# A batched lambda layer on Trainium2: the query matmul in quarters of the array, and one sum for all of them

## What is computed

```python
keys = xf @ Wk.T
softmax_keys = jax.nn.softmax(keys, axis=1)
values = _bn(xf @ Wv.T, gamma_v, beta_v, axes=(0, 2), ch_shape=(1, -1, 1))
queries = (xf @ Wq.T).reshape(b, n, k_dim, h).transpose(0, 2, 1, 3)
queries = _bn(queries, gamma_q, beta_q, axes=(0, 2, 3), ch_shape=(1, -1, 1, 1))
content_lambda = jnp.einsum('bmk,bmv->bkv', softmax_keys, values)
position_lambdas = jnp.einsum('nmk,bmv->bnkv', E, values)
content_output = jnp.einsum('bknh,bkv->bhvn', queries, content_lambda)
position_output = jnp.einsum('bknh,bnkv->bhvn', queries, position_lambdas)
return (content_output + position_output).reshape(b, d, n1, n2)
```

## Time and profile before

| | |
|---|---|
| median of 3 runs | 1535.9 us (1535.89 to 1537.47) |
| profiled execution | 1534.77 us, its span 1533.0 us |
| mean granted TensorE clock | 0.992 |
| PE / DVE / POOL / ACT busy | 1478.9 / 1004.7 / 681.2 / 420.0 us |

### The profile page before, as it was taken

The page is one execution under the profiler, slowest core; times in us unless marked ns, Lnnn a source line. Parts: engine busy times, 40 slices in busy tenths (PEclk is TensorE's granted clock), DMA queues, the critical chain, the costliest instruction groups (busy, mean ns, idle before and its releaser), DMA issues.

```text
span 1533.0 us, 28096 instructions
## 1 busy us (share of the span) xinstructions
PE 1478.9 (96%) x10443; PEld 1237.9 (81%) x10443; DVE 1004.7 (66%) x1416; ACT 420.0 (27%) x721; POOL 681.2 (44%) x524
## 2 busy tenths in 40 slices
PE   6886989999999999999999999999999999999997
PEld 6885768888888888888888888888888888888886
DVE  5769876666666666666666666666666666666663
ACT  4664322222222222222222222222222222222220
POOL 6663264444444444444444444444444444444441
PEclk9998999999999999999999999999999999999999
DMA  8744411625324341526233343416253243424221
GB/s 276 251 134 100 86 56 35 118 62 107 69 62 89 89 89 54 90 62 116 62 89 62 89 89 79 92 34 116 62 109 69 62 89 89 89 57 86 62 55 27
DMA packets 338460, 134.68 MB, mean 88 GB/s; under 512 B 202640, under 2 KB 333824, under 8 KB 337920
## 3 DMA queue, kind: packets, MB, share of 16 engines
q1 hardware_dynamic: 338432, 134.31, 39.4%
HBM read 109.12 MB, written 25.17 MB: 88 GB/s over the span
## 4 chain that ended last, share of the span: by engine, by line
PE 92%; DVE 5%; POOL 2%; issue 1%; ACT 0%; DMA 0%; DVEq 0%; SPq 0%; POOLq 0%; ACTq 0%
PE ps_a L1096 78%; PE ps_b L1113 8%; PE ps_b L989 3%; PE ps_a L979 1%; PE ps_a L1080 1%; DVE bn L676 1%; DVE q_stats L697 1%; POOL q_diag L475 0%; DVE e_lo L710 0%; DMA x_main<-in_x 0%; DVE v_nat L882 0%; DVE bn L679 0%; POOL s_buf L460 0%; DVE v_stats L691 0%; DVE pos L805 0%
## 5 line engine op out<-in xcount | busy, mean ns | idle before, releaser
L1096 PE MATMUL ps_a<-v_hi,e_hi 128*128 128x512 f32 x1736 | 683.1, 393 | 6.1 <-DVE pos L805 5.9
L1096 PE MATMUL ps_a<-v_hi,e_lo 128*128 128x512 f32 x1736 | 676.7, 390 | 0.0
L1096 PEld LDWEIGHTS ps_a<-v_hi,e_hi 128*128 128x128 f32 x1736 | 326.4, 188 | 76.5 <-issue 6.6
L1096 PE MATMUL ps_a<-b_lo,e_hi 128*128 128x512 f32 x992 | 386.5, 390 | 0.0
L1096 PEld LDWEIGHTS ps_a<-v_hi,e_lo 128*128 128x128 f32 x1736 | 326.6, 188 | 66.1
L569 ACT ACTIVATE e_hi<-e_nat 128x512 fp32r<-128x512 f32 x310 | 196.2, 633 | 595.2 <-PE ps_a L1096 588.5
L475 POOL TENSOR_TENSOR q_diag<-qn,row_mask 128x1024 f32<-128x1024 f32 x128 | 254.4, 2009 | 206.2 <-PE ps_b L1113 205.0
L471 POOL TENSOR_TENSOR e_nat<-e_nat,s_buf 128x512 f32<-128x512 f32 x62 | 81.0, 1306 | 523.5 <-DVE e_lo L705 523.5
L705 DVE TENSOR_TENSOR e_lo<-e_nat,e_hi 128x512 fp32r<-128x512 f32 x310 | 295.1, 952 | 0.3
L1096 PE MATMUL ps_a<-t_lo,e_hi 128*128 128x512 f32 x744 | 290.2, 390 | 0.0
L772 DVE TENSOR_TENSOR pos<-ps_a,content 128x512 f32<-128x512 f32 x186 | 128.7, 692 | 175.0 <-PE ps_a L1096 172.7
(11 more groups left out here) (126 smaller groups left out, 862.9 us busy)
## 6 DMA issues: line engine op xcount, KB each, us to landing
e_nat<-in_L_conv_E SPq DMA_DIRECT2D x128, 512.0 KB, 4.9
res<-in_x SPq DMA_DIRECT2D x64, 256.0 KB, 6.7
out_dram<-res SPq DMA_DIRECT2D x64, 256.0 KB, 4.8
x_main<-in_x SPq DMA_DIRECT2D x24, 512.0 KB, 4.6
q_dram<-q_nat SPq DMA_DIRECT2D x4, 2048.0 KB, 7.8
q_blk<-q_dram SPq DMA_DIRECT2D x32, 256.0 KB, 5.3
x_more<-in_x SPq DMA_DIRECT2D x8, 512.0 KB, 9.0
gam_q<-in_L_conv_gamma_q SPq DMA_DIRECT2D x8, 0.1 KB, 8.0
```

The lines of the kernel that those rows point to most:

```text
L1096: ins = nc.tensor.matmul(BANK_OF[i], e[:, i, j].rearrange("p n k -> p (n k)"), v[:, j], start=(STARTS[i] and j == 0 and n == 0), stop=(STO ...
```

## The change

The query takes one image in a matmul: 32 weight columns of `pos`, 32 columns of `q_diag`, in the quarter a of the array. There are 64 matmuls a pair instead of 32. Each result is wanted whole, and is written to columns (t, g) of its quarter of partitions, so that all results of a pair fill 512 columns of one PSUM bank, in the same order in all four quarters. `add_out` then makes one sum over 128 partitions instead of four over 32, except for the last pair, where four sums stay.

```diff
--- before.py
+++ after.py
@@ -810,15 +810,11 @@
                 if new_block:
                     dve.wait_ge(res_loaded, (p // PPB) * (16 * A) + 16 * A)
                 dve.wait_ge(queried, p + 1)
-                for a in range(A):
-                    rows = slice(a * V, (a + 1) * V)
-                    r = res[rows, :, bass.ds((p % (2 * PPB)) * (2 * TN), 2 * TN)].rearrange("v f (t n) -> v f t n", t=2)
-                    s = ps_b[rows, 0].rearrange("v (t a f n) -> v a f t n", t=2, a=2, n=TN)[:, a % 2]
-                    ins = nc.vector.tensor_tensor(r, s, r, ALU.add)
-                    if each:
-                        ins.then_inc(res_added, 1)
-                if not each:
-                    ins.then_inc(res_added, 1)
+                r = res[:, :, bass.ds((p % (2 * PPB)) * (2 * TN), 2 * TN)].rearrange("v f (t n) -> v f t n", t=2)
+                s = ps_b[:, 0, 0:BANK].rearrange("v (t f n) -> v f t n", t=2, n=TN)
+                for a in range(A if each else 1):
+                    rows = slice(a * V, (a + 1) * V) if each else slice(0, P)
+                    nc.vector.tensor_tensor(r[rows], s[rows], r[rows], ALU.add).then_inc(res_added, 1)
 
             def lam_scale():
                 dve.wait_ge(lam_summed, 1)
@@ -1106,10 +1102,9 @@
                     pe.wait_ge(res_added, p)
                 for t in range(2):
                     for g in range(G):
-                        for half in range(2):
-                            cols = slice(g * P + half * HALF, g * P + (half + 1) * HALF)
-                            to = ps_b[half * HALF:(half + 1) * HALF, 0, t * BANK:(t + 1) * BANK].rearrange(
-                                "v (a g f) -> v g a f", a=2, g=G)[:, g]
+                        for a in range(A):
+                            cols = slice((g * A + a) * V, (g * A + a + 1) * V)
+                            to = ps_b[a * V:(a + 1) * V, 0, (t * G + g) * V:(t * G + g + 1) * V]
                             ins = nc.tensor.matmul(to, pos[:, t, cols], q_diag[:, t, cols], start=True, stop=True)
                 ins.then_inc(queried, 1)
```

## The result

The changed kernel takes 1556.5 us (median of four runs, 1550.5 to 1562.6) against 1536.7 (four runs of the kernel before beside them): ratio 1.0127, interval 1.0105 to 1.0149. It is 20 us slower where 53 us less were forecast. The profiled execution took 1562.6 us, its span 1560.9.

A forecast was written before the change was run, and what follows sets the result against it. TensorE's issue was taken as the bound, its queries by weight loads. Savings of 52.9 + 0.1 = 53.0 us took the profiled 1534.77 to 1481.8, plus 1.1 for the median: 1483 us; 8-in-10 range 1475 to 1550, likeliest case 1476 to 1490.

The forecast's parts named there:

- Bound: Whole kernel: what TensorE issues sets the end; the query is bound by the weight load of each half.
- (a): Query matmuls: four quarters side by side, 31.7 ns a step, 1.03 us instead of 1.87; 52.9 us saved over 63 queries.
- (b): Feeding the query's records: between 7.9 and 29.2 ns a record; the sequencer's 4 ns an instruction favours the cheap end, taken.
- R1: Query on TensorE: each record costs a slot that doesn't shrink with width; +118 us, 1654 us; chance 0.13.
- R2: Query on TensorE: only two of four quarters overlap, 2.03 us a query; +10 us, 1546 us; chance 0.08.
- R3: Query's feeding: quarters only partly fed, 9 to 13 ns a record; 1491 to 1523 us; chance 0.12.
- (c): VectorE's sums: four become one, 130 us less DVE time, worth nothing on the path.
- (e): Who becomes late next: `head` keeps 0.4 us of cover, pairs last 20.44 us, nobody else comes near.
- (d): First sum before `query(1)`: it comes 2 us earlier, worth 0 to 0.15 us, taken as 0.1 us.
- R6: Query on TensorE: the change does not reach it, the query stays at 1.9 us; 1535 us; chance 0.05.
- R4: TensorE's loop code: 1184 matmul-side instructions grow to 1696 and are fetched each turn; +22 us, 1505 us; chance 0.04.
- R5: TensorE's clock: its sign was a clock under 1.00 in the steady windows; chance 0.03, size not in the text given.

The follow-up runs named there:

- shifted by 60: The changed kernel, its loop untouched, with 60 instructions of long-fulfilled waits put outside and ahead of TensorE's loop: 1488.4 us, ratio 0.9690.
- Shifted by 76: The changed kernel, its loop untouched, with 76 instructions of long-fulfilled waits put outside and ahead of TensorE's loop: 1500.8 us, ratio 0.9768.

## Why the prediction was wrong, point by point

**Bound, and parts (a) and (b): held, where the code is there.** A query lasts 1.10 us from first start to last (forecast 1.03, before 1.87), 8.6 ns a record. Its first four records start within 0.02 us of each other. R1 (14.6 ns and more), R2 (2.03 us) and R3 (9 to 13 ns) are out. A pair lasts 20.51 us against 20.44. The 0.07 us by 63 are 4.4 us, and the kernels whose loop is kept come out that much above the forecast: 1487.3 to 1488.4 against 1483. So the step of 31.7 ns for a quarter was undersized; (1.10 - 0.05) / 31 is 33.9.

**(c), the sum: held.** The two runs that differ in it alone are 1.3 us apart, within their intervals. **(e), who is late next: held.** In the unpaused pairs PE has no new wait. **(d)** is too small to be told apart. **R6** is out, the change reached TensorE.

**The step that failed is R4, the code.** The sum had put the code at nothing: the loop would be kept, as before. R4 named the other case, priced it at +22 us (1505) and gave it 0.04. The loop was fetched again, at some 73 us. Three things were wrong.

First the chance. "A loop is not fetched again in each turn" was read off 1184 matmul-side instructions, and the next size up was trusted to behave alike. The runs put the limit at seven blocks touched; eight were fetched again in six kernels of seven. By that count an estimate is 7 x 256 = 1792 instructions in the best place (the longest that was kept in seven blocks has 1763), and the changed loop would fit from 30 of 256 places.

Second the price. I took the bare transfer, 1.4 us, once a turn. There are nine fetches a jump back, nearly all hidden, and the one that isn't costs more than its transfer: the 14 late ones take 1.0 to 2.0 us, and the pauses cost 3.3 on average, with the 1.2 to 1.6 us between a fetch's end and the next matmul in them. The sequencer's 3.4 us at the jump are made alike (some 1.0 us until the fetch starts, 1.0 for it, 1.4 behind it), and hidden. The length of the jump is not what makes the branch long (3.4 to 5.8 us against 0.21): the kernel before jumps back over 1251 instructions, and the one shifted by 60 over 1763, in 0.21 us and without a fetch.

Third, what a pause sets off. R5 looked for a clock under 1.00 in the steady windows; it was 1.00 in the pairs of 20.51 us and fell behind the pauses instead: 12 of the 14 long ones left TensorE at half the clock for 3.4 or 6.8 us, which makes nearly all of the 1.9 us a turn beyond the pauses themselves. 14 turns by 5.2 us are 73 us. From 1487.3, the profiled execution of the kernel shifted by 60, to the 1562.6 of the changed one there are 75.

**Cover.** Part (b) looked at how fast the sequencer hands out instructions, not at how fast they come into it. A query of halves takes 1.87 us over 128 instructions; one of quarters takes 1.10 us over 256, one whole block, about the time of one fetch (1.1 us in the median, up to 2.3 in the changed kernel). In the changed kernel the query is numbers 3531 to 3786, so it ends 7 short of the border at 3793, and the block behind is asked for at 855.01, as it is needed. Shifted by 76, that border lies three quarters through the first query and the next but one just behind the second, and what is left is a pause of some 1 us or none. In the six-pair loop of halves, the second fetch is sent 2.8 us before the first query begins. That the place of the borders sets the price is shown by these runs (1556.5, 1500.8 and 1495.1 for one and the same loop, fetched again as often); how the chip chooses the moment of a fetch is not. Whether halves would pause in another place was not tried.

## What to carry to other kernels

When a change multiplies the instructions of an engine's loop, count them, and count the blocks of 256 that the loop touches (here seven were kept, eight in one kernel of seven), beside the arithmetic: fewer pairs in a turn cost nothing here (1536.8 against 1536.7) and kept the whole gain of 3.3%. More packets in the instruction queue (here 101 to 147 against 15 to 28) and a long branch at the loop's line (3.4 to 5.8 us against 0.21) were the mark of a loop that is fetched again; whether that costs time, only pauses show (with six pairs of halves both marks were there, and 1537.1 us). If a change is slower than its steps add up to, look for a period in the pauses before doubting the steps: one pair of four is a loop of four.

## What the runs showed of the hardware that I had not expected

- TensorE keeps a loop of 1763 instructions or not by where it begins: 60 idle instructions ahead of it are worth 68 us.
- The jump back of a loop that is fetched again holds the sequencer for 3.4 to 5.8 us (medians), a fetch of 16 KB itself lasting 0.9 to 2.6 us; in the changed kernel, sequencer and array go on only 1.2 to 1.6 us after the fetch's end. 17 matmuls of 512 columns that were still to start (4.0 us) hid branches of 3.3 to 3.6 us (those up to 3.9 but for 0.2), not those of 5.2 to 6.1; behind a quarter-wide query, whose last matmul had started 0.03 to 0.04 us before the branch, nothing was hidden.
- Four quarters of the array took plain fp32 records at 8.6 ns each on average (128 in 1.10 us), for 256 instructions in a row: 4.3 ns an instruction.
- A pause can cost more than itself. In the changed kernel TensorE ran at half the clock for 3.4 or 6.8 us behind 12 of 14 pauses (steps from start to start of 2.7 to 4.6 us; the two others were 2.4 and 3.5). With the jump right behind a query it did so behind all 13 (4.9 to 6.0 us), with the jump among the products and 80 instructions ahead behind 3 of 13 (1.8 to 2.6 us), and shifted by 76 behind none (up to 1.3 us).
